# Attention and SwiGLU block: eight PSUM banks, one of three for maxima products given to the scores

## The chip, the cores and the metric

One core of a Trainium2 chip runs the whole program. The metric is the time of one execution on the device in microseconds (us). Before the change it was 2622.42 us, the median of three runs (2621.76 to 2624.55).

## The reference

Four sequences of 1024 tokens with 512 channels go through one transformer layer, and the result is added to the input once more. All numbers are float32. The core of it:

```python
def _tc_rmsnorm(x, t, gw, gb, bw, bb):
    g = (t @ gw.T + gb)[:, None, :]
    b = (t @ bw.T + bb)[:, None, :]
    return g * x * jax.lax.rsqrt(jnp.mean(x * x, axis=-1, keepdims=True) + EPS) + b
def _attention(x, Wq, Wk, Wv, Wo):        # 16 heads of 32 channels
    attn = jnp.einsum('blhd,bmhd->bhlm', q, k) / scale
    o = jnp.einsum('bhlm,bmhd->blhd', softmax(attn), v).reshape(B, L, D)
    return o @ Wo.T
x1 = x + _attention(_tc_rmsnorm(x, ...), ...)
out = x + x1 + _swiglu(_tc_rmsnorm(x1, ...), gate_w, hid_w, out_w)   # hidden width 2048
```

## The kernel before

The program has two parts that run one after the other: `attention_program` for all four sequences (a loop over `b`), and then `ffn_program`. The change touches only the first. Every engine has its own stream of instructions, written out by hand in a fixed order, and the streams are tied together by semaphores. No engine reorders its work. Float32 products that need full precision are made of three products of parts (high x high, high x low, low x high), and that is why queries and keys exist as `_hi` and `_lo`.

**One sequence in attention.** First the V stage: eight tiles of values, each of twelve matmuls (line 899, recorded at the helper's line 776), copied from the bank to SBUF by ScalarE (line 537). Then eight units `u` (`NU`), each of four heads and half of the queries. A unit has eight steps `s` over blocks of 128 keys, and each step has four slots `h`, one for each head. Then the output stage: eight tiles of the output projection (line 941), copied by VectorE (line 758) and stored.

**One slot.** TensorE makes a 128 x 512 product of keys and queries (line 921, "the score"), ScalarE takes its exponential into `probs` (line 560). So that the softmax is stable, the maximum over the keys is subtracted before: it is added within the score product as extra rows of `qs` (partitions 96 to 127). For this the maxima of unit u+1 are worked out during unit u: in each slot TensorE makes one more product with queries and keys exchanged (line 838, "the maxima product"), and VectorE reduces it to one column (line 633, `pmax`). 32 such products make a unit's maxima. Those of unit 0 are made in the V stage (`MAX_IN_V`, from one to two after every three matmuls of the value tiles), those of unit 1 in the first 25 slots of unit 0 (`MAX_END`, so seven slots have two), and later ones one per slot, each unit's ending at slot 24 (step 6, head 0). Right behind the last one VectorE works the maxima into `mt` (lines 642, 646, 647), TensorE transposes `mt` at step 6, head 3 (line 824, behind that slot's maxima product), and ScalarE copies it to `qs` (line 452). The last unit, u = 7, has no maxima products.

**What else lies in the slots.** After the third or the fourth slot of a step TensorE multiplies the probabilities of the step before with V (line 861), and at every second step the sums of probabilities (made by GpSimd, line 409) with ones (line 849). Query and key projections of coming units are spread over the slots, three matmuls at a time (line 776), and are split to `qk_hi` by ScalarE (line 481) and `qk_lo` by VectorE (line 625). In step 3 VectorE normalises the unit before in four parts (`normalise`, lines 655, 658, 660, 663), one behind each slot's maximum. Units 5 and 7 also have the transposes of the next sequence (line 819), which ScalarE (lines 465, 469) and VectorE (line 621) work on.

**The banks.** PSUM has eight banks of 128 x 512. Bank 5 collects the output, bank 6 the denominators, bank 7 serves projections and transposes. Banks 0 to 4 are shared out by two constants:

```python
SB, MB = 2, 3
sbank = psum[0:SB]
mbank = psum[SB:SB + MB]
pe.wait_ge(st_done, SCORES_T(b, i + 1))      # before score i: the exponential of score i - SB has ended
pe.wait_ge(sq_done, SCORES_Q(b, n + 1))      # before maxima product n: the reduction of n - MB has ended
```

Value tiles use `sbank` too. The tiles of the output stage use `mbank`: tile t waits until tile t - MB has been copied out. Both waits stand ahead of the product's weight load, so whatever TensorE has in its stream behind them stands still with it.

Of the kernel before, what the change touches and what calls it, by code (L numbers as in the profile page):

```python
# [40 lines left out]

HT_AT = {5: (10, 14, 18, 22), 7: (0, 4, 8, 12)}
MAXIMA_AT = (6, 3)
SB, MB = 2, 3
NMAX = GH * TPH * NHALF
V_ALONE = (2 * KT, 6)
MAX_END = 25
# [1362 lines left out]
```

## Time and profile before

| | us |
|---|---|
| median of three runs | 2622.42 |
| profiled execution, as timed | 2623.54 |
| its span in the profile | 2621.7 |
| TensorE busy | 2474.9 (94%) |
| VectorE busy | 1478.8 (56%) |
| ScalarE busy | 1261.1 (48%) |
| GpSimd busy | 755.0 (29%) |

The profile is one execution. Times are us from the span's start. PE is TensorE's matmuls, PEld its weight loads, DVE is VectorE, ACT is ScalarE, POOL is GpSimd. A number in brackets with an arrow is the idle time of the engine just before an instruction, and what ended it. Matmuls are pipelined: in a free stream a new weight load starts every 0.23 us although each matmul is shown as 0.4 us, so a stall of the stream is best read from the starts of the weight loads.

### The profile page before, as it was taken

What the parts mean: (1) busy time and instruction counts of PE and PEld (TensorE: products, weight loads), DVE (VectorE), ACT (ScalarE), POOL (GpSimd) and SP (SyncE); (2) the same over time, 40 slices, a digit from 0 to 9 for tenths busy, and PEclk for the clock granted to TensorE, in tenths of its full rate; (3) what the DMA queues carried; (4) which work ended last, traced back from release to release, by engine and by line L of the source; (5) the groups of instructions that cost most, each with busy time, mean ns of one, the idle gap of its engine ahead of it and who ended that gap; (6) DMA issues with size and microseconds to landing.
All of it is one profiled execution on the core that took longest, in us unless ns stands there. A gap on an engine that the chain in (4) does not pass through costs nothing. (4 is left out here: it accounts for less than half of the span.)

```text
span 2621.7 us, 38622 instructions
## 1 busy us (share of the span) xinstructions
PE 2474.9 (94%) x11764; PEld 1651.4 (63%) x11764; DVE 1478.8 (56%) x2316; ACT 1261.1 (48%) x2206; POOL 755.0 (29%) x557
## 2 busy tenths in 40 slices
PE   5999989999989999899999869999999999999999
PEld 4644437544446544365444448888888888888887
DVE  4766735667736667446677354554545454545454
ACT  4455662566653556625566524344434333343343
POOL 0255550455541555514555510000101010101010
PEclk8999999999999999999999979999999999999999
DMA  5222103212132112032121260101010101000000
GB/s 197 49 47 55 57 13 102 49 45 58 45 93 53 42 43 64 29 102 46 40 65 45 87 271 1 49 1 50 1 49 1 48 3 38 12 24 27 17 33 17
DMA packets 56685, 135.18 MB, mean 52 GB/s; under 512 B 11664, under 2 KB 11664, under 8 KB 53136
## 3 DMA queue, kind: packets, MB, share of 16 engines
q1 hardware_dynamic: 55920, 130.34, 16.7%
q8 instruction: 113, 1.85, 0.3%
q0 software_dynamic: 544, 2.10, 0.2%
q14 instruction: 108, 0.88, 0.1%
HBM read 59.78 MB, written 19.92 MB: 30 GB/s over the span
## 5 line engine op out<-in xcount | busy, mean ns | idle before, releaser
L409 POOL TENSOR_TENSOR sums<-probs 128x512 f32<-128x512 f32 x512 | 653.1, 1301 | 790.2 <-ACT probs L560 788.5
L633 DVE TENSOR_REDUCE pmax<-bank 128x1 f32<-128x512 f32 x1024 | 655.0, 685 | 279.5 <-PE bank L838 268.3
L560 ACT ACTIVATE probs<-bank 128x512 f32<-128x512 f32 x1024 | 584.1, 597 | 403.8 <-PE bank L921 370.2
L921 PE MATMUL bank<-qs,ks 128*128 128x512 f32 x1024 | 458.9, 453 | 29.2 <-ACT probs L560 28.5
L921 PEld LDWEIGHTS bank<-qs,ks 128*128 128x128 f32 x1024 | 191.3, 188 | 373.0 <-ACT probs L560 225.4
L838 PE MATMUL bank<-ks,qs 96*128 96x512 f32 x1024 | 401.1, 404 | 25.6 <-DVE pmax L633 25.5
L1306 PE MATMUL bank<-h_hi,gu_hi 128*128 128x512 f32 x1024 | 400.1, 391 | 9.3 <-DVE h_lo L1183 4.8
L1306 PE MATMUL bank<-h_hi,gu_lo 128*128 128x512 f32 x1024 | 399.5, 390 | 0.0
L1306 PE MATMUL bank<-h_lo,gu_hi 128*128 128x512 f32 x1024 | 399.4, 390 | 0.0
L1217 DVE TENSOR_TENSOR sg<-bank,sg 128x512 f32<-128x512 f32 x128 | 88.5, 691 | 385.2 <-PE bank L1306 385.2
L861 PE MATMUL bank<-probs,v 128*32 128x512 f32 x2048 | 275.9, 611 | 8.0 <-ACT o L492 5.3
L1139 ACT ACTIVATE a_hi<-sg 128x512 fp32r<-128x512 f32 x128 | 80.9, 632 | 386.9 <-DVE sg L1217 386.9
L838 PEld LDWEIGHTS bank<-ks,qs 96*128 96x128 f32 x1024 | 193.8, 189 | 73.0 <-DVE pmax L633 46.7
L1084 POOL TENSOR_TENSOR x<-x,res 128x2048 f32<-128x2048 f32 x8 | 38.2, 4770 | 668.5 <-DMA x<-attn_out 668.5
L1306 PEld LDWEIGHTS bank<-h_hi,gu_hi 128*128 128x128 f32 x1024 | 192.9, 188 | 51.5 <-issue 11.4
L1306 PEld LDWEIGHTS bank<-h_hi,gu_lo 128*128 128x128 f32 x1024 | 192.9, 188 | 40.2
L1306 PEld LDWEIGHTS bank<-h_lo,gu_hi 128*128 128x128 f32 x1024 | 192.9, 188 | 39.9
L1287 PE MATMUL bank<-wo_hi,a_hi 128*128 128x512 f32 x512 | 202.5, 396 | 0.0
L1287 PE MATMUL bank<-wo_hi,a_lo 128*128 128x512 f32 x512 | 199.6, 390 | 0.0
L1287 PE MATMUL bank<-wo_lo,a_hi 128*128 128x512 f32 x512 | 199.2, 389 | 0.0
L1189 DVE TENSOR_TENSOR gu_lo<-wT,gu_hi 128x512 fp32r<-128x512 f32 x258 | 188.2, 771 | 11.7 <-ACT gu_hi L1113 9.9
L1137 ACT ACTIVATE sg<-bank 128x512 f32<-128x512 f32 x128 | 76.3, 596 | 244.9 <-PE bank L1306 244.9
(108 smaller groups left out, 2767.4 us busy)
## 6 DMA issues: line engine op xcount, KB each, us to landing
ks<-qk_hi SPq DMA_DIRECT2D x136, 128.0 KB, 2.4
qs<-qk_hi SPq DMA_DIRECT2D x264, 64.0 KB, 2.0
x<-in_x SPq DMA_DIRECT2D x10, 1024.0 KB, 5.5
ks<-qk_lo SPq DMA_DIRECT2D x68, 128.0 KB, 2.4
qs<-qk_lo SPq DMA_DIRECT2D x132, 64.0 KB, 2.0
wv<-wv_parts SPq DMA_DIRECT2D x4, 2048.0 KB, 9.1
attn_out<-yout SPq DMA_DIRECT2D x32, 256.0 KB, 2.6
wT<-in_gu_w SPq DMA_DIRECT2D x8, 1024.0 KB, 14.2
```

What stands on the lines that cost most here:

```text
L409: nc.gpsimd.tensor_tensor(sums[:, h, :], probs[:, 0, h, :], probs[:, 1, h, :], ALU.add) \
L560: nc.scalar.activation(probs[:, s % 2, h, :], sbank[i % SB][:], ACT.Exp, scale=SCALE).then_inc(st_done, 1)
L633: nc.vector.reduce_max(pmax[:, t, h, hf:hf + 1], mbank[n % MB][:], AX_X).then_inc(sq_done, 1)
L838: nc.tensor.matmul(mbank[n % MB][:], qs[0:96, u % 3, h, t * P:(t + 1) * P], ks[0:96, u // 2 % 2, h, hf * QB:(hf + 1) * QB], start=True, st ...
L861: last = nc.tensor.matmul(obank[DH * h:DH * h + DH, :], v[:, s, (g * GH + h) * DH:(g * GH + h + 1) * DH], probs[:, s % 2, h, :], start=(s ...
L921: nc.tensor.matmul(sbank[i % SB][:], ks[:, g % 2, h, s * P:(s + 1) * P], qs[:, u % 3, h, :], start=True, stop=True).then_inc(st_ready, 1)
L1137: nc.scalar.activation(sg[:, j % 2, :], psum[n % GU_BANKS][:], ACT.Silu).then_inc(g_act, 1)
L1139: nc.scalar.activation(a[0][:, j % 2, :], sg[:, j % 2, :], ACT.Copy).then_inc(ah, 1)
L1189: nc.vector.tensor_tensor(gu[1][:, slot, w, :, :], wT[:, j, w, :, :], gu[0][:, slot, w, :, :].bitcast(F32), ALU.subtract).then_inc(gul, 1)
L1217: nc.vector.tensor_tensor(sg[:, j % 2, :], psum[n % GU_BANKS][:], sg[:, j % 2, :], ALU.mult).then_inc(prod, 1)
L1287: last = nc.tensor.matmul(ybank[t][:], a[p][:, j % 2, t * P:(t + 1) * P], wo[q][:, j % 2, :], start=(j == 0 and p == 0 and q == 0), stop=( ...
L1306: last = nc.tensor.matmul(psum[n % GU_BANKS][:], gu[p][:, j % 2, w, k, :], hT[q][:, hf, k, :], start=(i == 0), stop=(i == len(steps) - 1))
```

## The change

One line changes. `sbank` becomes banks 0 to 2 and `mbank` banks 3 and 4. The semaphore counts that depend on the two constants (starting values and targets) follow from them. No instruction is added, removed or moved.

```diff
-SB, MB = 2, 3
+SB, MB = 3, 2
```

## Rows read from the trace of the kernel before

**Rows 1.** Busy time by stage; columns: stretch, length, each engine's busy time, PEclk, DMA share, GB/s.
```profile
425.00:461.00 36.00, 35.03 (x152) 27.73 (x152) 21.34 (x37) 7.30 (x11) 0.00 (x0) 1.00 0.12 30
461.00:723.00 262.00, 249.57 (x1293) 124.82 (x1291) 180.62 (x297) 163.47 (x286) 139.92 (x112) 1.00 0.20 49
723.00:758.00 35.00, 30.36 (x164) 13.60 (x168) 6.85 (x9) 25.43 (x46) 20.75 (x17) 1.00 0.10 23
...
1520.00:2621.00 1101.00, 1069.27 (x4759) 883.17 (x4757) 562.17 (x819) 424.44 (x758) 89.56 (x25) 0.99 0.09 36
```

**Rows 2.** Scores, line 921: idle time of the weight-load and matmul rows together, us, times.
```profile
  ACT probs L560: 253.9, 468
```

**Rows 3.** Maxima products, line 838: the same.
```profile
  DVE pmax L633: 72.2, 108
```

**Rows 4.** Waits of TensorE's matmuls: us in total, times, longest.
```profile
PE bank L921 <- ACT probs L560: 28.5, 60, 1.3
PE bank L838 <- DVE pmax L633: 25.5, 40, 1.6
```

**Rows 5.** Timeline of a stretch of three slots in unit 3, second sequence: PEld, DVE.
```profile
588.49 0.19 PEld L921 LDWEIGHTS bank<-qs,ks 128*128 128x128 f32 x1 [0.42 <-ACT probs L560]
588.60 0.19 PEld L838 LDWEIGHTS bank<-ks,qs 96*128 96x128 f32 x1
589.15 0.16 PEld L861 LDWEIGHTS bank<-probs,v 128*32 128x32 f32 x8 [0.36 <-ACT probs L560]
...
588.08 0.69 DVE L633 TENSOR_REDUCE pmax<-bank 128x1 f32<-128x512 f32 x1 [1.83 <-PE bank L838]
```

**Rows 6.** Timeline of the next five slots, with the normalisation: PEld, DVE.
```profile
592.66 0.19 PEld L838 LDWEIGHTS bank<-ks,qs 96*128 96x128 f32 x1 [0.59 <-DVE pmax L633]
...
594.80 0.19 PEld L838 LDWEIGHTS bank<-ks,qs 96*128 96x128 f32 x1 [1.14 <-DVE pmax L633]
...
591.91 0.69 DVE L633 TENSOR_REDUCE pmax<-bank 128x1 f32<-128x512 f32 x1
592.52 1.63 DVE L663 TENSOR_TENSOR o<-o,den 128x512 f32<-128x512 f32 x1
594.07 1.87 DVE L633 TENSOR_REDUCE pmax<-bank 128x1 f32<-128x512 f32 x3
```

**Rows 7.** Timeline at step 6 of the same unit: PEld, DVE.
```profile
604.80 0.57 PEld L824 LDWEIGHTS bank<-identr,mt 128*128 128x128 f32 x4
...
604.59 1.88 DVE L633 TENSOR_REDUCE pmax<-bank 128x1 f32<-128x512 f32 x3
```

**Rows 8.** Timeline in unit 0: PEld, then DVE.
```profile
480.38 0.42 PEld L838 LDWEIGHTS bank<-ks,qs 96*128 96x128 f32 x2
...
481.62 2.48 DVE L633 TENSOR_REDUCE pmax<-bank 128x1 f32<-128x512 f32 x4
```

**Rows 9.** Timeline of VectorE in the V stage.
```profile
436.58 5.62 DVE L633 TENSOR_REDUCE pmax<-bank 128x1 f32<-128x512 f32 x9
```

**Rows 10.** Timeline in the output stage of the first sequence: DVE.
```profile
405.99 0.69 DVE L758 COPY yout<-bank 128x512 f32<-128x512 f32 x1
...
413.61 0.69 DVE L758 COPY yout<-bank 128x512 f32<-128x512 f32 x1 [4.43 <-DMA attn_out<-yout]
```

**Rows 11.** Waits of the weight loads in unit 7, second sequence: us, times, longest.
```profile
PEld bank L921 <- ACT probs L560: 12.2, 20, 1.6
```

**Rows 12.** Timeline of GpSimd in unit 7.
```profile
732.29 3.74 POOL L409 TENSOR_TENSOR sums<-probs 128x512 f32<-128x512 f32 x3 [0.95 <-ACT probs L560]
```

**Rows 13.** Busy time by stage in unit 5, first and second sequence; columns as rows 1.
```profile
300.00:305.00 5.00, 3.40 (x18) 1.59 (x21) 4.70 (x8) 3.02 (x6) 1.90 (x2) 0.93 0.00 0
305.00:310.00 5.00, 5.00 (x26) 2.06 (x22) 2.92 (x5) 2.07 (x5) 1.32 (x2) 0.73 0.00 0
...
673.00:678.00 5.00, 5.00 (x30) 2.32 (x22) 3.27 (x6) 3.67 (x7) 3.08 (x3) 1.00 0.11 13
```

## Prediction

> **What bounds the kernel now.** I read the busy time by stage first. From 1520 us on the feed-forward part runs, with TensorE busy 1069 of 1101 us [rows 1]. It uses none of the two constants, so all that follows is about the four sequences before it, some 365 us each. In one of them TensorE is busy 35.0 of 36 us in the V stage, 249.6 of 262 us in units 0 to 6, and 30.4 of 35 us in unit 7 [rows 1]. It is the bound on average, yet VectorE has 180.6 us and ScalarE 163.5 us in units 0 to 6, so neither could be the bound on average, only in bursts.
>
> The bursts are the point. Two neighbouring score and maxima products take 0.46 us of a free TensorE stream, while a reduction follows the one before in 0.60 us (nine in 5.62 us [rows 9]). So each run of slots between two value products outpaces its readers, and banks decide how long TensorE may run ahead. The two rows of idle time show the present balance: scores waited for exponentials 468 times of 1024 for 253.9 us in the weight-load and matmul rows together [rows 2], maxima products for reductions 108 times for 72.2 us [rows 3]. These overstate the loss: most of it lies beside matmuls still in the pipe, and the matmul rows alone have 28.5 and 25.5 us [rows 4]. So neither total is used as a price. I walked the starts of the weight loads instead, stretch by stretch.
>
> **The rule of the walk.** A product of line 838 may start 0.06 us after its bank's reduction ends (reduction 591.91 + 0.69 = 592.60, load 592.66 [rows 6]). With MB = 2 that is the reduction of the last but one product, not of the last but two. A score then asks for the exponential three before, which in the stretches I walked had always ended well before the score's place came, so the score waits go. After a stall the next load follows in 0.11 instead of 0.23 us (588.49 to 588.60 [rows 5]), which gives back 0.12 us.
>
> **Three slots without projection.** Now the third score waits until 588.49, its maxima product loads at 588.60, the values at 589.15. With two banks its partner is the first product of the stretch, whose reduction ends at 588.08 + 0.69 = 588.77 [rows 5]. Afterwards the score goes earlier, but the maxima product must load at 588.82, values at about 589.25: 0.10 us later, although the score wait is gone. The reason is that the maxima product comes second in a slot, and its reader takes longer. Five slots without projection come out at 0 to +0.1 us in the same way, and slots with a projection behind each (three loads of 0.23 us) at 0. I count three of 0.10 us a unit in units 0 to 6, so 2.1 us a sequence.
>
> **Normalisation.** In step 3 VectorE has four more operations between its reductions. Now the fourth product loads at 592.66 and the fifth at 594.80. With two banks the third, which now waits for nothing and loads over 1 us earlier, must wait for the reduction at 591.91, hence 592.65; the fourth for the first of the three at 594.07, which ends at 594.75, hence 594.80 [rows 6]. Behind it come three projection loads and a score, the fifth product at 595.85 (0.11 + 4 x 0.23 later), and the values 1.17 us later than now. GpSimd's sums lie beside the 1.63 us of line 663. The same walk gives 1.17 us in units 1 and 3, 0.60 in units 2 and 4, 1.0 in unit 5 and 0.6 in unit 6: 5.1 us a sequence.
>
> **The chain of maxima.** At step 6 VectorE works out `mt` behind the last maximum, and three maxima products of the next unit lie on TensorE before the transposes of `mt` (line 824). Three banks take all three without a reduction; two don't. Now the transposes load at 604.80, right behind the third. With MB = 2 it waits for the first reduction behind the chain, 604.59 + 0.68 = 605.27, so it loads at 605.32 and the transposes at 605.43 or later [rows 7]. That is 0.63 us here and 0.7 in the even units; I take 0.7 in units 0 to 5: 4.3 us (unit 6 has no product left there).
>
> **Unit 0 and V stage.** Slots with two maxima products have their second one held. In one such slot both load from 480.38 on while VectorE still waits for a projection's `qk_lo`; the second would wait for the first of four reductions from 481.62 on, till 482.36 [rows 8]. The walk of unit 0 gives 0.66, 0.85, 0.59 and 0.59 us: 2.7 us. In the V stage VectorE is saturated with 0.60 us a reduction [rows 9], which two banks can still feed; what is added is the in-order stall of each second product of a pair, alternately 1.20 and 1.40 us a pair where now 1.20, so 0.10 us for 14 pairs: 1.4 us.
>
> **Output stage.** Tile 2 now follows tile 1 at once. With two banks it waits for the copy of tile 0, 405.99 + 0.69 = 406.68. The copy of tile 2 waits for a store behind the 2 MB load of `wv`, till 413.61 [rows 10], and tile 4 for that copy, till 414.36. From there four tiles follow, where now three follow from about 0.7 us later; a tile takes some 2.7 us, less that 0.7 us: the walk ends 2.1 us later.
>
> **The gains.** In unit 7 the maxima are absent and the third score bank is a gain alone: 12.2 us of weight-load waits, the longest of 1.6 us [rows 11]. What is late next is GpSimd: three sums take 3.74 us [rows 12], and the denominators (line 849) wait for four of them. By the walk the first denominator product gains 0.6 us, the third some 2.1, the end some 3.0. Above it could be 5 us (TensorE idle in unit 7 is 35 - 30.4 = 4.6 [rows 1]), below 1. The end of unit 6, where ScalarE copies the maxima's rows, gives 0.75 more.
>
> **The clock.** In unit 5 of the first sequence TensorE was busy 3.40 us of 5, and then the granted clock fell to 0.73 over the next 5 us; at the same place of the second sequence it stayed at 1.00 [rows 13]. Since a low stretch is granted 1.2 instead of 2.4 GHz, 0.27 x 5 + 0.07 x 5 = 1.7 us were lost. New stalls of 1 to 2 us turn up in each unit's normalisation, stalls in unit 7 go. I take two or three more such stretches in all, 4 us; the bounds are -5 and +30 us.
>
> **The sum.** A sequence: 2.1 + 5.1 + 4.3 + 2.7 + 1.4 + 2.1 - 3.0 - 0.75 = 13.95 us. Four: 55.8 us, with the clock about 60. The profiled execution's own time was 2623.5 us, which gives 2683; the median shown lies 1.1 us lower, so 2682 us.
>
> **Rivals.** *Scores first (faster).* If the maxima waits hid under matmuls in the pipe, as the small 25.5 us [rows 4] may suggest, only the gains are left: 3.75 us a sequence and what score waits cost in units 0 to 6, at most TensorE's idle time there, 262 - 249.6 = 12.4 us [rows 1]. That is 3.75 to 16 us a sequence, 2558 to 2607 us; I take 8, so 2590. The Trainium skill (Perfetto Trace Analysis, Optimization Strategy) says that a gap which repeats on the engine that should be saturated can mean too few PSUM buffers for the next tile. By that rule the side with 468 waits [rows 2] is the one short of banks. The trace agrees that the gap repeats; the walk says that the bank only moves the gap by one instruction. Chance 7%.
>
> *A trade.* The two waits replace each other more evenly than by the walk, because later slots catch up what step 3 and step 6 lose; then V stage, short stretches and output stage stay (5.6 us) beside the gains (3.75): 4 x 1.85 = 7 us, and 2630 us. Against it: the value products close each stretch, and TensorE has next to no idle time behind them to catch up in. Chance 10%.
>
> *The clock decides (slower still).* If half of the 28 places of normalisation and of the maxima chain bring a low stretch, 14 to 18 x 1.7 = 24 to 30 us come on top: 2705 us. The Trainium skill (TensorE: Matmul & The Clock Gate, A second HAM failure mode: psum-queue depth-cycling) tells of a kernel whose short idle times between groups of matmuls, from cycling through banks, made the clock oscillate. Of this the trace has unit 5's one case in two. Chance 18%.
>
> *No effect.* The loads might be gated by something else, so that bank counts don't matter; against it stand the loads that follow a reduction's end by 0.06 us [rows 6]. Chance 3%, 2622 us.
>
> The forecast itself, 2682 us with 2660 to 2698, has 62%. About 0.2% (5 us) is what a measurement can tell from no change here. Faster 0.07, same 0.05 (no effect and the low end of the trade), slower 0.88. The range reaches to the clock's case and part way to the trade: 2645 to 2710 us.
>
> **What would show it.** After: waits of scores for exponentials nearly gone in units 0 to 6; waits of maxima products for reductions up from 108 to 400 or more; units 1 to 4 longer by 1.7 to 2.1 us each; unit 0 by some 3.5; unit 7 shorter by about 3; the output stage 2 us longer. Feed-forward unchanged. The prediction is wrong if units 1 to 4 keep their length or unit 7 gains nothing.

## Result and profile after

The changed kernel takes 2722.3 us (median of four runs, 2713.8 to 2724.7) against 2623.5 us for the kernel before, 1.0364 times as long (95% interval 1.035 to 1.0379): 99 us slower. Slower had been forecast, but 2682 us, and the time lies above the range (2645 to 2710). The profiled execution took 2713.8 us with a span of 2712.0, 90.3 more than before, with a mean granted clock of 0.976 where it had been 0.987.

The busy time by stage of the second sequence is the view that explains most. Its columns are those of rows 1; the stages are the V stage, units 0 to 7 and the output stage. After:

```profile
444.50:485.10 40.60, 38.65 (x156) 27.88 (x157) 23.21 (x38) 7.31 (x11) 0.00 (x0) 1.00 0.11 27
485.10:526.00 40.90, 36.60 (x181) 19.00 (x180) 26.56 (x43) 21.32 (x36) 16.67 (x14) 1.00 0.26 59
526.00:567.20 41.20, 37.69 (x189) 18.87 (x188) 25.81 (x41) 22.02 (x38) 20.11 (x17) 0.96 0.08 20
567.20:606.70 39.50, 36.42 (x189) 18.47 (x188) 25.37 (x41) 21.92 (x39) 20.07 (x17) 1.00 0.27 61
606.70:646.40 39.70, 36.24 (x189) 18.48 (x188) 25.80 (x41) 22.04 (x39) 20.15 (x17) 1.00 0.17 47
646.40:689.50 43.10, 39.70 (x189) 19.60 (x189) 27.98 (x48) 24.29 (x47) 21.09 (x18) 0.92 0.25 56
689.50:733.30 43.80, 38.62 (x194) 18.83 (x193) 28.47 (x44) 26.86 (x46) 21.04 (x17) 0.92 0.15 43
733.30:769.80 36.50, 32.50 (x171) 14.88 (x169) 23.41 (x39) 23.22 (x45) 20.65 (x17) 1.00 0.08 30
769.80:802.80 33.00, 29.36 (x168) 13.41 (x168) 7.34 (x10) 25.38 (x46) 21.42 (x17) 1.00 0.11 25
802.80:833.80 31.00, 26.98 (x117) 19.30 (x113) 13.00 (x20) 5.99 (x10) 3.96 (x3) 0.94 0.60 179
```

The same cuts in the kernel before have the lengths in the table. The granted clock there was 1.00 in every stage but the output stage (0.94). "Forecast" is the walk of the prediction, "clock" what a granted clock under 1.00 took in the stage after (length x (1 - PEclk)).

| stage | before | after | change | forecast | of it clock |
|---|---|---|---|---|---|
| V stage | 37.3 | 40.6 | +3.3 | +1.4 | 0 |
| unit 0 | 37.0 | 40.9 | +3.9 | +3.7 | 0 |
| unit 1 | 37.7 | 41.2 | +3.5 | +2.2 | 1.6 |
| unit 2 | 37.7 | 39.5 | +1.8 | +1.6 | 0 |
| unit 3 | 37.7 | 39.7 | +2.0 | +2.2 | 0 |
| unit 4 | 37.9 | 43.1 | +5.2 | +1.6 | 3.4 |
| unit 5 | 38.6 | 43.8 | +5.2 | +2.0 | 3.5 |
| unit 6 | 36.2 | 36.5 | +0.3 | +0.2 | 0 |
| unit 7 | 35.2 | 33.0 | -2.2 | -3.0 | 0 |
| output | 29.2 | 31.0 | +1.8 | +2.1 | 0 more |
| sum | 364.5 | 389.3 | +24.8 | +14.0 | 8.5 |

Every unit that ran at full clock lies within 0.3 us of its walk, except unit 7. What the clock took is an estimate; with it taken off, units 1, 4 and 5 come out at +1.9, +1.8 and +1.7 us, within 0.3 us of the walk too. What is missing in the forecast is the clock (8.5 us here) and over half of the V stage (1.9 us).

The waits answer rows 2 and 3. First the idle time ahead of the scores (line 921), then ahead of the maxima products (line 838), weight-load and matmul rows together:

```profile
  ACT probs L560: 99.4, 136
```

```profile
  DVE pmax L633: 342.9, 474
```

The scores' waits fell from 468 to 136, those of the maxima products rose from 108 to 474. In units 0 to 6 of the second sequence the scores' waits went from 96 (49.9 us) to 22 (17.3 us): fewer, but not nearly gone as forecast. The waits of the matmuls alone (rows 4) went from 25.5 us to this, and the scores' row there, 28.5 us before, has fallen below the others:

```profile
PE bank L838 <- DVE pmax L633: 96.7, 100, 2.3
```

The place where it happens is the one walked in [rows 6]. The timeline of unit 3 of the changed kernel, weight loads and then VectorE:

```profile
626.60 0.19 PEld L838 LDWEIGHTS bank<-ks,qs 96*128 96x128 f32 x1 [1.13 <-DVE pmax L633]
...
628.75 0.19 PEld L838 LDWEIGHTS bank<-ks,qs 96*128 96x128 f32 x1 [1.84 <-DVE pmax L633]
...
629.78 0.19 PEld L838 LDWEIGHTS bank<-ks,qs 96*128 96x128 f32 x1
630.34 0.16 PEld L861 LDWEIGHTS bank<-probs,v 128*32 128x32 f32 x8 [0.37 <-issue]
...
625.86 0.69 DVE L633 TENSOR_REDUCE pmax<-bank 128x1 f32<-128x512 f32 x1
626.47 1.62 DVE L663 TENSOR_TENSOR o<-o,den 128x512 f32<-128x512 f32 x1
628.01 1.96 DVE L633 TENSOR_REDUCE pmax<-bank 128x1 f32<-128x512 f32 x3
```

The third product loads 0.05 us after the reduction that ends at 626.55, the fourth behind the first of the three (628.01 + 0.69), the fifth 1.03 us later without a wait, the values at 630.34: the order of events that had been walked. The chain of maxima at step 6 also goes as walked: the third product now waits out `mt`, and the transposes stand behind it:

```profile
640.42 0.19 PEld L838 LDWEIGHTS bank<-ks,qs 96*128 96x128 f32 x1 [1.59 <-DVE pmax L633]
640.72 0.52 PEld L824 LDWEIGHTS bank<-identr,mt 128*128 128x128 f32 x4
```

Whether the single terms of the walk have the right size can be read from the value products (line 861), which close each step: a step is taken here from the first weight load of one to that of the next. Of unit 3 before, behind the one at 589.15 in [rows 5]:

```profile
595.23 0.16 PEld L861 LDWEIGHTS bank<-probs,v 128*32 128x32 f32 x8 [0.24 <-issue]
600.10 0.16 PEld L861 LDWEIGHTS bank<-probs,v 128*32 128x32 f32 x8 [0.37 <-ACT probs L560]
605.45 0.16 PEld L861 LDWEIGHTS bank<-probs,v 128*32 128x32 f32 x8
```

and after:

```profile
623.20 0.16 PEld L861 LDWEIGHTS bank<-probs,v 128*32 128x32 f32 x8 [0.24 <-issue]
630.34 0.16 PEld L861 LDWEIGHTS bank<-probs,v 128*32 128x32 f32 x8 [0.37 <-issue]
635.19 0.16 PEld L861 LDWEIGHTS bank<-probs,v 128*32 128x32 f32 x8 [0.36 <-ACT probs L560]
641.31 0.16 PEld L861 LDWEIGHTS bank<-probs,v 128*32 128x32 f32 x8
```

The step with the normalisation took 6.08 us (589.15 to 595.23) and takes 7.14: 1.06 more, for 1.17 in the walk. The step with the chain took 5.35 us and takes 6.12: 0.77 more, for 0.63. Over all sequences, where neither kernel had a low clock, the normalisation's step grew by 1.05, 0.60, 1.05, 0.60 and 0.49 us in units 1, 2, 3, 4 and 6 (walk: 1.17, 0.60, 1.17, 0.60, 0.6), and the chain's by 0.72 to 1.05 us in units 1 to 5 (walk: 0.7).

### The profile page after: what moved, and what is told of

Same layout as the page of the kernel before. It is cut to its first block and busy times, and to the rows that moved or that the text cites. A ratio compares the mean times of both kernels' runs of the same rounds, so it can differ in the third digit from the quotient of the medians.

```text
span 2712.0 us, 38622 instructions
## 1 busy us (share of the span) xinstructions
PE 2504.7 (92%) x11764; PEld 1657.8 (61%) x11764; DVE 1487.8 (55%) x2316; ACT 1253.0 (46%) x2206; POOL 754.6 (28%) x557
## 5 line engine op out<-in xcount | busy, mean ns | idle before, releaser
L633 DVE TENSOR_REDUCE pmax<-bank 128x1 f32<-128x512 f32 x1024 | 673.8, 687 | 357.3 <-PE bank L838 347.4
L560 ACT ACTIVATE probs<-bank 128x512 f32<-128x512 f32 x1024 | 575.3, 597 | 463.2 <-PE bank L921 443.4
L838 PE MATMUL bank<-ks,qs 96*128 96x512 f32 x1024 | 438.8, 435 | 106.3 <-DVE pmax L633 96.7
L921 PE MATMUL bank<-qs,ks 128*128 128x512 f32 x1024 | 430.4, 429 | 2.8 <-ACT probs L560 2.6
L861 PE MATMUL bank<-probs,v 128*32 128x512 f32 x2048 | 287.1, 634 | 9.1 <-ACT o L492 6.4
L1306 PEld LDWEIGHTS bank<-h_hi,gu_lo 128*128 128x128 f32 x1024 | 192.5, 188 | 40.1
L1189 DVE TENSOR_TENSOR gu_lo<-wT,gu_hi 128x512 fp32r<-128x512 f32 x258 | 166.0, 684 | 10.4 <-ACT gu_hi L1113 8.5
```

The source lines that it names most:

```text
L560: nc.scalar.activation(probs[:, s % 2, h, :], sbank[i % SB][:], ACT.Exp, scale=SCALE).then_inc(st_done, 1)
L633: nc.vector.reduce_max(pmax[:, t, h, hf:hf + 1], mbank[n % MB][:], AX_X).then_inc(sq_done, 1)
L838: nc.tensor.matmul(mbank[n % MB][:], qs[0:96, u % 3, h, t * P:(t + 1) * P], ks[0:96, u // 2 % 2, h, hf * QB:(hf + 1) * QB], start=True, st ...
L861: last = nc.tensor.matmul(obank[DH * h:DH * h + DH, :], v[:, s, (g * GH + h) * DH:(g * GH + h + 1) * DH], probs[:, s % 2, h, :], start=(s ...
L921: nc.tensor.matmul(sbank[i % SB][:], ks[:, g % 2, h, s * P:(s + 1) * P], qs[:, u % 3, h, :], start=True, stop=True).then_inc(st_ready, 1)
L1189: nc.vector.tensor_tensor(gu[1][:, slot, w, :, :], wT[:, j, w, :, :], gu[0][:, slot, w, :, :].bitcast(F32), ALU.subtract).then_inc(gul, 1)
```

## Experiments

Theory A is the prediction's: TensorE stands still, in order, behind maxima products whose bank isn't reduced yet, and the third score bank pays only where there are no maxima. The rivals are in each expectation. All experiments were timed beside the kernel before on the same chip (2625.2 to 2625.9 us there, so differences between two experiments of a few us are within what the runs scatter).

**The bank taken, and given to nobody.**

```diff
-SB, MB = 2, 3
+SB, MB = 2, 2
```

> SB, MB = 2, 2: the bank is taken from the maxima products and given to nobody. Theory A (the loss is TensorE standing still in order behind maxima products whose bank isn't reduced yet; the third score bank gives back some 4 us a sequence, in unit 7 and at the end of unit 6): 2722 + 4 x 4 = 2738 us, 2730 to 2750. Rival B (the third score bank hides much of the loss in units 0 to 6 as well, since 468 scores waited): over 2770 us. Rival C (the third score bank is worth nothing): 2722 us.

Measured: 2730.2 us (2723.8 to 2736.5), ratio 1.0391 (1.0365 to 1.0417). The medians put the third score bank at about 8 us of the whole kernel, where 16 had been expected, and the range of theory A (from 2730) just holds the time. The intervals of the two ratios overlap, so the times alone exclude neither rival C nor the 16 us. The profile says where the difference lies. Units 1 and 7 of the second sequence with two and two banks:

```profile
530.60:570.30 39.70, 36.73 (x189) 18.51 (x188) 25.82 (x41) 22.35 (x38) 20.09 (x17) 1.00 0.09 20
...
775.30:810.50 35.20, 30.54 (x168) 13.53 (x168) 7.07 (x10) 25.42 (x45) 20.96 (x17) 1.00 0.10 23
```

Unit 1 takes 39.7 us, as its like, unit 3, does in the changed kernel. From one value product (line 861) to the next the two kernels agree within 0.08 us, mostly within 0.03, in each of the 145 steps of units 0 to 5 in which both had the full clock. Only the end of unit 6 (37.0 us against 36.5) and unit 7 (35.2 against 33.0) gain. Beside two maxima banks, then, the third score bank is worth nothing in units 0 to 5: the scores wait less (362 times here, 136 there), and the reductions set the same pace. Rival B is out. A third score bank beside three for the maxima, which would need a sixth bank, wasn't run.

**The normalisation spread out**, in the changed kernel and in the kernel before.

```diff
+NORM_AT = [(3, 0), (3, 3), (4, 2), (5, 1)]
...
-                            if s == 3 and u:
-                                normalise(b, u - 1, h)
+                            if (s, h) in NORM_AT and u:
+                                normalise(b, u - 1, NORM_AT.index((s, h)))
```

> The changed kernel (3 and 2), with the four parts of the normalisation behind slots 12, 15, 18 and 21 of a unit in place of 12, 13, 14 and 15. Theory A: the maxima products of slots 17 and 18 stood 1.8 to 3.5 us in each of units 1 to 6; of this some 0.6 to 1.2 us a unit goes (5.1 us a sequence), and with the long stalls two of the six or so low-clock stretches of a sequence (1.7 us each): 2722 - 4 x 8.5 = 2688 us, 2675 to 2702. Rival (VectorE has the same sum of work, a place in its stream doesn't matter): within 5 us of 2722.

> The kernel before (2 and 3), normalisation spread in the same way. Theory A: with three banks only 0.2 to 1.6 us of stalls at slots 18 and 19 of units 1 to 6 are there to be removed, and score waits take part of their place: 2623 - 4 x 3 = 2611 us, 2603 to 2619. Rival (three banks had covered it already): within 3 us of 2623.

Measured: 2688.8 us for the changed kernel with it (ratio 1.0246, 1.0225 to 1.0266), 33.5 us less than without, and 2604.6 us for the kernel before with it (0.9918, 0.9899 to 0.9936), 20.6 us less. Both times lie in theory A's ranges, and VectorE did the same work in both. In the changed kernel unit 3 goes from 39.7 to 37.9 us and unit 6 from 36.5 to 35.0 at full clock:

```profile
601.80:639.70 37.90, 36.20 (x190) 18.41 (x189) 26.03 (x41) 21.99 (x38) 20.56 (x17) 1.00 0.19 50
...
723.80:758.80 35.00, 32.34 (x172) 14.96 (x170) 23.39 (x39) 23.22 (x45) 20.94 (x18) 1.00 0.08 31
```

Unit 2 stayed (39.5 and 39.6). It would be wrong to take the 1.8 us of units 1 and 3 for the price of the missing bank, because the kernel with three maxima banks gains nearly as much. There unit 3 goes from 37.7 to 36.2 us:

```profile
563.50:599.70 36.20, 35.75 (x189) 18.28 (x188) 25.56 (x41) 22.26 (x39) 20.59 (x17) 1.00 0.19 52
```

So with the normalisation spread the bank still costs 1.7 us in unit 3, where it cost 2.0. The term of the step itself falls from 1.06 to 0.52 us (5.07 against 4.55 us between value products), but part of it comes back in the step with the chain (0.98 in place of 0.77). Three banks hadn't covered the normalisation either. By span and mean clock both kernels gain some 22 us at full clock (an estimate: 2712.0 x 0.976 against 2687.0 x 0.977, and 2621.7 x 0.987 against 2602.3 x 0.986). That the changed kernel came out near its 2688 us is in part luck: the forecast counted 3.4 us a sequence for low-clock stretches that go, and the mean clock hardly moved (0.976 to 0.977). Of the 99 us between the one sharing of the banks and the other, 84 stay.

This kernel also bounds what the scores' waits cost before. They are as many and as long as in the kernel before (466 for 254.7 us, against 468 for 253.9), yet TensorE is busy 35.75 of 36.20 us in unit 3. That is a hint and no proof, since a score's matmul that stood is shown longer (476 ns in the median here, 399 in the changed kernel).

**The third bank lent only where there are no maxima.** In the kernel before, from step 7 of unit 6 on, the scores rotate over banks 2, 0 and 1 and wait for the exponential three before.

```diff
+LENT = 2
+LEND_FROM = NT + ((NU - 2) * NS + 7) * GH
...
+    def score_bank(i):
+        if i >= LEND_FROM:
+            return (psum[LENT], sbank[0], sbank[1])[(i - LEND_FROM) % 3]
+        return sbank[i % SB]
...
-                            pe.wait_ge(st_done, SCORES_T(b, i + 1))
-                            nc.tensor.matmul(sbank[i % SB][:], ks[:, g % 2, h, s * P:(s + 1) * P],
+                            pe.wait_ge(st_done, SCORES_T(b, i + 1 - (i >= LEND_FROM)))
+                            nc.tensor.matmul(score_bank(i)[:], ks[:, g % 2, h, s * P:(s + 1) * P],
```

> The kernel before (2 and 3), but from step 7 of unit 6 on, when no maxima product is left in the sequence, the scores rotate over three banks, the third lent by the maxima. It does only the part of the change that theory A counts as gain. Theory A: unit 7 goes from 35.2 to about 33 us, the end of unit 6 gives 0.7 us: 2623 - 4 x 3.5 = 2609 us, 2603 to 2614. Rival (the gain of unit 7 is given back in the output stage, where stores and the load of wv set the pace): 2618 to 2623 us.

Measured: 2610.3 us (2607.4 to 2614.0), ratio 0.9939 (0.9919 to 0.9958), 15 us less than before. Unit 7 takes 32.9 us, as in the changed kernel, and unit 6 35.8 us where it took 36.2. The lines of these two units:

```profile
683.80:719.60 35.80, 32.76 (x170) 14.62 (x170) 23.23 (x39) 23.51 (x45) 20.62 (x18) 1.00 0.08 30
719.60:752.50 32.90, 29.31 (x168) 13.39 (x168) 7.36 (x10) 25.24 (x46) 21.36 (x17) 1.00 0.11 25
```

The output stage took back 0.5 us of these 2.7 (29.7 us, before 29.2), so that the second sequence as a whole is 2.2 us shorter, which would be 9 us in four. The span of the profiled execution is 9.5 us shorter, and the median's 15 has an interval of 11 to 21 us. This is the gain that the change had to offer, without its price.

**The clock by itself.** With two and two banks one bank is free. Matmuls into it, which nobody reads, stand right ahead of the maxima products that had stood longest, and fill less than the stall.

```diff
+ODD, EVEN = {17: 3, 18: 6, 27: 2}, {18: 4, 27: 5}
+FILL = [{6: 3, 8: 2, 11: 2, 17: 6, 21: 2, 24: 2, 27: 3}, ODD, EVEN, ODD, EVEN, {17: 8, 18: 3, 25: 5, 27: 3}, {17: 2, 18: 6}, {}]
...
+                            for _ in range(FILL[u].get(s * GH + h, 0)):
+                                nc.tensor.matmul(psum[4][:], identr[:], wq[0][:, 0, :], start=True, stop=True)
                             for n in next_maxima(u, s, h):
                                 max_tile(b, NMAX + n)
```

> The kernel with two and two banks (2730 us), with 87 matmuls a sequence added whose product goes into the bank that is free there and is read by nobody. They stand right ahead of the maxima products that stood longest (slots 17, 18, 25 and 27), two to eight in one place, and fill less than the stall found there (35 us of stalls a sequence against 87 x 0.23 = 20 us). The waits stay as they are; only TensorE isn't idle in them. Theory D (idle stretches in front of the maxima products bring the low clock, some 15 more stretches of 3.4 us in units 0 to 6 than the kernel before): the low stretches in these units go, and though work is added the time falls by some 15 x 1.7 = 25 us, to 2705 us, 2695 to 2715. Rival (the low clock comes from something else, the load as a whole): the low stretches stay, 2730 to 2745 us.

Measured: 2714.9 us (2706.5 to 2721.0), ratio 1.0328 (1.0302 to 1.0354), against 2730.2 without the added matmuls. The intervals of the two ratios don't meet, and the profiles show where it comes from. Units 0 to 5 of the second sequence, first with two and two banks, then with the matmuls added:

```profile
492.60:741.80 249.20, 230.34 (x1120) 112.61 (x1118) 160.23 (x259) 139.76 (x242) 122.54 (x97) 0.95 0.20 50
```

```profile
490.80:730.80 240.00, 236.99 (x1201) 124.09 (x1201) 160.33 (x259) 139.77 (x241) 122.77 (x97) 1.00 0.21 52
```

In the four sequences together this stretch fell from 990.6 to 959.7 us, and its granted clock from 0.95 to 0.97 up to 1.00 in each. One by one, units 3 to 5 of the second sequence with two and two banks:

```profile
611.40:653.90 42.50, 39.52 (x190) 19.50 (x188) 25.83 (x41) 22.37 (x38) 20.14 (x17) 0.92 0.15 44
653.90:693.80 39.90, 37.16 (x190) 18.53 (x188) 28.02 (x48) 24.52 (x46) 21.06 (x18) 1.00 0.27 60
693.80:738.30 44.50, 40.64 (x194) 19.09 (x192) 28.46 (x44) 27.33 (x45) 21.00 (x17) 0.88 0.14 42
```

and the same with the matmuls added, then units 6 and 7:

```profile
606.90:646.70 39.80, 39.29 (x201) 20.54 (x199) 25.85 (x41) 22.34 (x38) 20.18 (x17) 1.00 0.18 47
646.70:686.70 40.00, 39.32 (x199) 20.06 (x197) 28.03 (x48) 24.53 (x46) 21.10 (x18) 1.00 0.27 60
686.70:727.30 40.60, 40.35 (x213) 21.32 (x211) 28.48 (x44) 27.36 (x45) 21.10 (x17) 1.00 0.16 46
727.30:765.90 38.60, 37.13 (x179) 16.66 (x177) 23.44 (x39) 23.98 (x45) 21.01 (x18) 0.96 0.08 28
765.90:802.70 36.80, 32.17 (x168) 13.89 (x167) 6.97 (x10) 25.40 (x45) 20.93 (x17) 0.95 0.10 22
```

With more matmuls (213 records in unit 5 in place of 194) unit 5 is 3.9 us shorter, since the clock stays at 1.00. It was the idle time that brought the clock down, not the load. It is no remedy as a whole. Units 0 to 5 gave 31 us, more than the 25 expected, but the low clock turned up in units 6 and 7, which had been free of it, and the last output stage and the feed-forward part, where no matmul was added, took 8 us more in this execution (1139.7 us from the last value product on, against 1131.6; why isn't known). So the median is 15 us lower and not 25. Unit 5 at full clock gives the stalls' own price: 40.6 us against 38.6 before, the 2.0 us of the walk.

**Fewer pairs in the V stage**, in the changed kernel.

```diff
-V_ALONE = (2 * KT, 6)
+V_ALONE = (KT, 6)
```

> The changed kernel (3 and 2), with the 32 maxima products of the V stage spread over 22 quarters of value tiles in place of 18, beginning four quarters earlier: 12 quarters have one, 10 have two (4 and 14 before). The changed kernel's V stage is 3.2 us longer than with three banks, where 1.4 had been worked out. Theory A (two banks serve a reduction every 0.64 us where VectorE alone needs 0.60, and each pair stalls the stream behind it): with fewer pairs 1.5 to 3 us of a V stage go, 2722 - 4 x 2.2 = 2713 us, 2708 to 2718. Rival (it is VectorE's sum of work that sets the V stage): within 3 us of 2722.

Measured: 2715.0 us (2709.5 to 2720.2), ratio 1.0346 (1.0324 to 1.0368). That is 7 us less than the changed kernel. The intervals overlap, so the time alone doesn't show it. V stage and output stage of the second sequence are 40.6 + 31.0 = 71.6 us for the changed kernel and 44.1 + 25.7 = 69.8 us here (with the maxima the cut between the output stage and the next V stage lies earlier), 1.8 us less a sequence. It fits the 1.5 to 3 us of theory A, at their low end.

**The chain of maxima**, with slots 25 to 27 left free in the changed kernel.

```diff
-MAX_AT = spread(NMAX, MAX_END) + [1] * ((NU - 2) * NMAX) + [0] * (NU * NS * GH - MAX_END - (NU - 2) * NMAX)
+MAX_AT = spread(NMAX, MAX_END) + ([0] * 3 + spread(NMAX, UNIT - 3)) * (NU - 2) + [0] * (NU * NS * GH - MAX_END - (NU - 2) * UNIT)
```

> The changed kernel (3 and 2), but slots 25, 26 and 27 of units 0 to 5 have no maxima product; the 32 of a unit lie in the 29 other slots, so three slots have two. Theory A (the third product behind the last maximum stands until VectorE has made mt, 1.5 to 2.0 us at slot 27, 0.7 us net, and the transposes of mt with it): 0.7 x 6 a sequence goes, three pairs a unit cost 0.1 to 0.3 each, and some low-clock stretches go: 2722 - 4 x (4.2 - 2.5) - 8 = 2707 us, 2695 to 2718. Rival (the pairs cost as much as the chain): 2719 to 2730 us.

Measured: 2726.8 us (2723.3 to 2730.1), ratio 1.038 (1.0357 to 1.0403). A miss: the rival's number. Unit 0, which has its pairs anyway, is 0.8 us shorter (40.1 in place of 40.9 us), which is the chain's 0.7; unit 3 with three new pairs is 0.8 us longer (40.5 in place of 39.7). If the chain's 0.7 us went in unit 3 too, the three pairs cost 1.5 us there, some 0.5 each and not 0.1 to 0.3. They don't cost alike: the step with the first pair alone is 0.8 us longer in unit 3, and the step with the chain doesn't get shorter there at all, which fits the third pair, in slot 24, right before it. So the chain's term shows in unit 0 alone.

**The order within a slot**, in the changed kernel.

```diff
+                            for n in next_maxima(u, s, h):
+                                max_tile(b, NMAX + n)
                             pe.wait_ge(st_done, SCORES_T(b, i + 1))
                             nc.tensor.matmul(sbank[i % SB][:], ks[:, g % 2, h, s * P:(s + 1) * P],
                                              qs[:, u % 3, h, :], start=True, stop=True).then_inc(st_ready, 1)
-                            for n in next_maxima(u, s, h):
-                                max_tile(b, NMAX + n)
```

> The changed kernel (3 and 2) with the two products of each slot exchanged: the maxima product first, the score behind it. Theory A (the loss of the short stretches comes from the maxima product being second in its slot: its bank is asked for 0.11 us behind the score, and its reduction starts as much later): where a stretch ends in a stalled pair, the stalled product now has the free score behind it, and a stretch ends about as late or 0.1 us earlier, some five stretches a unit: 2722 - 4 x 7 x 0.5 = 2708 us, 2698 to 2718. Rival (it is the reductions' pace alone that sets a stretch, whichever product is first): within 4 us of 2722.

Measured: 2721.2 us (2717.6 to 2731.6), ratio 1.0381 (1.0352 to 1.0411): nothing. Units 1 and 3 (39.2 and 39.1 us) are some 0.6 us shorter than unit 3 of the changed kernel, and unit 6 0.7 us, but unit 0 is 0.4 us longer and unit 5 1.5 us, the latter by its clock (0.89 in place of 0.92). What units 1, 3 and 6 gain lies in the step with the normalisation (0.8 us); the short stretches, for which the edit was made, are not shorter (0 to 0.1 us longer). So their 0.1 us is real, but the reason given in the prediction, that the maxima product is second in its slot, isn't borne out.

**A version that beats both.** The kernel before with the normalisation spread and the bank lent:

> The kernel before (2 and 3) with both edits that made it faster: the normalisation behind slots 12, 15, 18 and 21 (2604.6 us alone), and the third bank lent to the scores from step 7 of unit 6 on (2610.3 alone). They touch different units, so by theory A they add up: 2623 - 20 - 15 = 2590 us, 2584 to 2596. Rival (unit 7 has the normalisation of unit 6 too, and its late parts hold up the output stage, which now comes earlier): 2596 to 2604 us.

Measured: 2591.9 us (2587.9 to 2596.9), ratio 0.987 (0.9845 to 0.9894), 34 us less than before, where the edits alone gave 20.6 and 14.9. The two edits add up. With the V stage's maxima begun earlier as well:

> The kernel with both edits (2 and 3, normalisation spread, third bank lent from step 7 of unit 6 on; 2592 us), and the maxima products of the V stage begun four quarters earlier (22 quarters in place of 18). Theory A: with three banks the V stage has only 1.2 us of stalls left in it, of which half goes: 2592 - 4 x 0.7 = 2589 us, 2585 to 2592. Rival (the earlier products collide with the output tiles of the sequence before, on VectorE and in the banks): 2593 to 2600 us.

Measured: 2588.7 us (2583.4 to 2591.5), ratio 0.986 (0.9835 to 0.9885), 1.4% faster than the kernel before and 4.9% faster than the changed one. The 3 us between these two are expected but within their intervals.

## Why the prediction was right and wrong

**Bound and rule of the walk: right.** TensorE in order was the bound, the feed-forward part didn't move (1131.3 us from the last value product to the end before, 1130.7 after), and a maxima product that stood loads 0.05 us after the reduction of the last but one. With two maxima banks a third score bank gives nothing in units 0 to 5 and pays only from step 7 of unit 6 on, where lending it gave 15 us. That the scores weren't short of a bank beside three maxima banks is argued from TensorE's busy time in the spread kernel (35.75 of 36.20 us in unit 3 with the same score waits), and isn't shown by a run.

**Normalisation, chain, unit 0, short stretches: right in size.** Units at full clock came out at +3.9, +1.8, +2.0, +0.3 (units 0, 2, 3, 6) for +3.7, +1.6, +2.2, +0.2, and unit 5 at +2.0 for +2.0 once added matmuls held the clock. The starts of the value products bear out the single terms as well (normalisation 1.05 for 1.17, chain 0.77 for 0.63 in unit 3). Two things that the prediction suggests don't hold: the normalisation's stalls aren't the work of the missing bank alone, since spreading it gained 20.6 us with three banks too, and the reason put forward for the short stretches fell in the exchange of the two products. Two slips of the prediction are small: six times 0.7 us are 4.2 and not 4.3, and 594.80 + 0.11 + 4 x 0.23 is 595.83.

**V stage: mis-sized, +3.3 us for +1.4.** The failed step is that two banks "can still feed" a VectorE with 0.60 us a reduction. The walk priced only TensorE's stalls there (0.10 us a pair) and put what they do to VectorE at nothing. Of the changed kernel's V stage, weight loads and then VectorE:

```profile
461.49 0.19 PEld L838 LDWEIGHTS bank<-ks,qs 96*128 96x128 f32 x1 [0.17 <-DVE pmax L633]
462.09 0.19 PEld L838 LDWEIGHTS bank<-ks,qs 96*128 96x128 f32 x1 [0.41 <-DVE pmax L633]
462.19 0.42 PEld L776 LDWEIGHTS bank<-wv,hT_hi 128*128 128x128 f32 x2
462.67 0.19 PEld L776 LDWEIGHTS bank<-wv,hT_lo 128*128 128x128 f32 x1
462.90 0.19 PEld L838 LDWEIGHTS bank<-ks,qs 96*128 96x128 f32 x1
...
460.75 2.57 DVE L633 TENSOR_REDUCE pmax<-bank 128x1 f32<-128x512 f32 x4 [0.24 <-PE bank L838]
463.56 0.69 DVE L633 TENSOR_REDUCE pmax<-bank 128x1 f32<-128x512 f32 x1 [0.24 <-PE bank L838]
```

The reduction at 460.75 ends at 461.44, its bank's next product loads at 461.49. The product that stood until 462.09 is reduced last of the four, from 463.32 - 0.69 = 462.63 on, 0.54 us behind its load. A bank in turn thus needs 0.05 + 0.54 + 0.69 = 1.28 us, so two banks give a reduction every 0.64 us, and the four take 2.57 us, 0.09 more than four in 2.48 us [rows 8]. The stall reaches VectorE a second time: the value tile's three loads stand behind it, so the next maxima product loads only at 462.90, its reduction starts at 463.56, and the engine idles 0.24 us. From 460.75 to 463.56 there are four reductions in 2.81 us, 0.70 each, where nine took 5.62 us [rows 9], 0.62 each. So two banks do slow the reader itself, besides stalling the stream: VectorE needs 25.6 us from the first to the last start of the 32 reductions, where it needed 22.4. Four V stages: 4 x 1.9 = 8 us of the miss.

**Unit 7 and the gains: a little too large.** -2.2 us for -3.0 in unit 7. The kernel that lends the bank ends at the same 32.9 us. GpSimd is late next, as forecast: the weight loads of line 849 waited 18.1 us for its sums in the whole trace after, in 12 places.

**Output stage: near.** +1.8 us for +2.1 in the second sequence. From a sequence's last value product to the next one's first, the V stage included, it took 71.0, 72.4 and 71.4 us before and takes 78.2, 78.1 and 77.0, so 5.6 to 7.2 us more; the output stage isn't resolved further.

**The clock: the step that failed, and most of the miss.** The prediction took two or three more low stretches in all, 4 us. Worked out from mean clock and span, the loss is 0.013 x 2621.7 = 34 us before and 0.024 x 2712.0 = 65 us after: 31 us for 4. That is the size that had been given to the rival "the clock decides" (24 to 30 us, 18%), and its time of 2705 us plus the V stage's 8 us is 2713, what the profiled execution took (the fastest of the four; their median is 2722.3). The failed step is the choice between the bounds -5 and +30. The one pair of places in [rows 13] said that a stall of that length brings the low clock in one case of two; the walk itself put a stall of 1 to 2 us into the normalisation of six units, 24 places in four sequences, and a shorter one into the chain of six units, 24 more (the rival's 28 places undercount them). One in two of these is 12 to 24 more low stretches, not two or three; 31 us at 1.7 us each are 18. The trace after shows how one comes about. Three stretches of 5 us in unit 1:

```profile
540.00:545.00 5.00, 4.90 (x27) 2.00 (x19) 3.47 (x6) 2.60 (x5) 3.20 (x3) 1.00 0.44 102
545.00:550.00 5.00, 2.90 (x9) 1.63 (x8) 4.11 (x5) 1.41 (x4) 1.78 (x2) 0.88 0.02 3
550.00:555.00 5.00, 5.00 (x26) 2.23 (x26) 1.43 (x3) 1.39 (x3) 0.69 (x1) 0.78 0.00 0
```

In the normalisation, where two maxima products stood 1.13 us (until 545.85) and 1.83 us (until 547.99), TensorE was busy 2.90 us of 5, and the clock fell right behind, when there was work again. The same stall stands in each unit, yet unit 3 kept its clock and unit 1 didn't; what decides between two equal stalls stays open here. That the stalls cause it is shown by the added matmuls, which removed every clock loss in units 0 to 5 of all four sequences. The Trainium skill (TensorE: Matmul & The Clock Gate, A second HAM failure mode: psum-queue depth-cycling) describes short idle times from cycling through banks that make the clock oscillate. The trace agrees with it: behind the stalls of 1.13 and 1.83 us the granted clock was 0.88 and 0.78, and in unit 2 it was 1.00 again.

The Trainium skill (Perfetto Trace Analysis, Optimization Strategy) says that repeated gaps can mean too few PSUM buffers, and this had spoken for the change. Taking a bank from the maxima products did cost some 100 us, but the side with the longer row of waits, 468 against 108, was not the one that could use it: beside two maxima banks the scores' third bank gave nothing in units 0 to 5.

Put together for the profiled execution: 4 x 14 us of walk, 4 x 1.9 of V stage and 31 of clock make 95 us, and unit 7's smaller gain (4 x 0.8) 98; the spans differ by 90.3. The rest of 8 us isn't traced.

## What to carry to other kernels

When two in-order streams share a pool of banks, don't read the shortage from the number of waits: take each wait's place, and ask which instruction sets the next one's start once it is gone. A lump of other work on the reader can cost whatever the number of banks: here spreading it gave 20.6 us with three and 33.5 us with two, and needed no bank. To tell what a bank covers from what it doesn't, make the same edit in both kernels. A bank can be lent for the part of the program in which its owner has nothing to do. And price a new stall of TensorE twice, once as idle time and once for the clock behind it: here the second was a third of the whole loss (31 of 90 us).

## What the runs showed of the hardware

Added matmuls whose result nobody reads made a kernel faster, 2730.2 to 2714.9 us, because the granted clock of units 0 to 5 went from 0.95 to 0.97 up to 1.00 in each sequence. The low clock then came in units 6 and 7, which had been free of it (0.96 and 0.95). Stalls of equal length brought it in unit 1 and not in unit 3. With two banks in turn a reduction of 128 x 512, of which nine in a row had taken 0.62 us each, came every 0.64 to 0.70 us: its bank was loaded for again 0.05 us after it had ended, and the next reduction from that bank started 0.54 us after that load.
